# A two-layer graph network: 500 more tiles of edges counted in stage two, stored blocks' products placed early

## The chip, the cores and the metric

The kernel runs on one core of a Trainium2 chip. It is judged by its device time in microseconds, the median of several executions.

## What is computed

The graph has 12500 nodes with 128 features and 400000 edges, sorted by destination; a destination is 12500 times the square of a uniform number, so low nodes have most edges. Cut to what matters:

```python
def _mean_agg(h, src, dst, deg_inv):
    summed = jax.ops.segment_sum(h[src], dst, num_segments=N_NODES)
    return summed * deg_inv[:, None]
def _sage_conv(h, src, dst, deg_inv, W_self, W_neigh, b):
    return h @ W_self + _mean_agg(h, src, dst, deg_inv) @ W_neigh + b
h = jax.nn.relu(_sage_conv(x, src, dst, deg_inv, W_self1, W_neigh1, b1))
x = _layernorm(x + _sage_conv(h, src, dst, deg_inv, W_self2, W_neigh2, b2))
ef = (jax.nn.relu(edge_attr @ We1 + be1) @ We2 + be2) * jax.nn.sigmoid(ts @ Wt + bt)
msg = jax.nn.relu(jnp.concatenate([x[row], ef], axis=1) @ Wn1 + bn1) @ Wn2 + bn2
out = _layernorm(x + x + jax.ops.segment_sum(msg, col, num_segments=12500))
```

## The kernel before

Three stages run one after the other, with prefixes in the profile's names: `sum_x_` (sums over neighbours of x, then the nodes' first layer), `sum_z_` (the same with z, the first layer's result in the form of the second), `messages_` (the edges' part). The edges stand in tiles of 128, 3125 of them, five tiles to a group, 625 groups.

**Two ways to sum.** *Gathered* groups: POOL fetches for each tile 128 rows of the table by index (L954, an indirect DMA of 64 KB), DVE makes a one-hot matrix of destinations in a window of 64 nodes (L855), PE multiplies both (L1040, in fp32, which is two passes a tile), and DVE adds the window to `sums` (L1170). *Counted* tiles: the first 1250 (`COUNTED`), with the most edges for a node, are cut into 17 blocks. For every block a matrix is made that counts how often each of its up to 128 nodes has each source node: DVE makes two one-hot matrices of a tile (L1225 by destination and upper part of the source, up to 5 nodes x 98 columns; L1220 by its lower seven bits, five tiles at a time), PE multiplies them (L1051), DVE adds what the tile before left in a shared column (L1236, the carry), and ACT copies the result into `counts` (L1121). ACT clears these first (L1110). When a block is complete its counts are multiplied with the whole table: 98 matmuls with 384 columns (385 in stage 1), since the table is split into three bf16 parts (L1064). The table streams through a ring of three chunks, 14 chunks a product (L1014). The product is copied (ACT L1154), turned with six matmul passes (PE L1072) and added (DVE L1181).

**Stages.** Stage 1 (`counting=True`) counts the 1250 tiles, stores each block's counts in DRAM (3136 KB each) and gathers the other 375 groups. Stage 2 makes no counts: it loads the 17 stored ones (L1004, into two buffers in turn), multiplies them with its own table, and gathers the same 375 groups. Beside this, pieces of 256 nodes go through 15 steps each (`second_nodes` in stage 2: mean, two small products, layer norm, stores of y and rest), 49 pieces. Stage 3 gathers for all 625 groups; its edge indices `src_idx` and places `rel` are loaded and converted within stage 2.

**Order.** Nothing is scheduled by a program: every engine runs through slots `s = 0, 1, ...`, one for a group, and the plan (`make_plan`) says which tiles, products and pieces stand in a slot. Both stages have 375 groups and 401 slots. The tiles of stage 1 are spread over 340 slots by cost; in stage 2 a product takes 18 slots, one begins every 19 (`loaded_by`). POOL may be ten groups ahead of PE: it waits for `sums_ready`, which PE raises after a group's last window. SP issues all loads in program order and stands at a chunk until PE has freed one of the three. Within a slot PE mixes windows, counts and product evenly (lines 1079 to 1095).

## Time and profile before

| | us |
|---|---|
| Median of 3 executions | 10677.33 (10667.98 to 10677.83) |
| The profiled execution, in all | 10652.36 |
| Its span | 10648.5 |
| Granted TensorE clock, mean | 0.725 of full speed |

Busy in the whole span: PE 58%, PEld 46% (weight loads, beside PE), DVE 36%, ACT 25%, POOL 61%. The three stages lie one behind the other in the trace: stage 1 ends at 3099, stage 2 at 5888, stage 3 with the span. A busy POOL means an indirect DMA being written (0.94 us each); the time between two of them does not count as busy, though 0.30 us of it is always there. The clock and the DMA share must be read by stretch, since stage 2 differs from the other two.

### The profile page before, as it was taken

The numbers are of one execution on the slowest core, as the hardware profiler recorded it, in microseconds if no ns is written. First come the engines' busy times: TensorE is split into PE (matmuls) and PEld (weight loads), VectorE is DVE, ScalarE is ACT, GpSimd is POOL, SyncE is SP. The second block draws the span as 40 slices with busy tenths as digits, with TensorE's granted clock in tenths as the row PEclk, the third lists the DMA queues.
The fourth block names the chain that finished last, engine by engine and source line by source line (L and its number), as shares of the span: only waits on it lengthen the run. The fifth ranks groups of instructions, "written<-read, shape, count | busy, mean of one in ns | idle before, by whom it ended". The sixth has DMA issues, their size and how long they took to land. (4 is left out here: it accounts for less than half of the span.)

```text
span 10648.5 us, 114426 instructions
## 1 busy us (share of the span) xinstructions
PE 6164.5 (58%) x31767; PEld 4857.4 (46%) x31767; DVE 3810.3 (36%) x9118; ACT 2663.4 (25%) x3928; POOL 6516.8 (61%) x6882
## 2 busy tenths in 40 slices
PE   3456566666643334444444567666766667676676
PEld 2344444444433333343333455545555555555555
DVE  6766666666520111111111223233333333333333
ACT  3433333333200000000000233333333333333333
POOL 5555556566646666666665566666666666666665
PEclk9855666777756666666665788888888878888888
DMA  2334444555524444444432333333333333333332
GB/s 71 88 98 124 125 141 152 156 163 179 175 93 144 158 135 148 150 152 148 152 102 56 112 109 109 110 110 110 111 111 110 112 111 113 112 113 119 107 122 91
DMA packets 568848, 1305.10 MB, mean 123 GB/s; under 512 B 161231, under 2 KB 374499, under 8 KB 547476
## 3 DMA queue, kind: packets, MB, share of 16 engines
q1 hardware_dynamic: 348209, 846.63, 23.4%
q0 software_dynamic: 220000, 451.00, 15.7%
q8 instruction: 273, 4.47, 0.2%
q14 instruction: 366, 3.00, 0.1%
HBM read 1190.99 MB, written 106.10 MB: 122 GB/s over the span
## 5 line engine op out<-in xcount | busy, mean ns | idle before, releaser
L1465 POOL DMA_INDIRECT messages_rows<-y_d,src_idx x3125 | 2948.0, 943 | 1825.8 <-issue 955.4
L954 POOL DMA_INDIRECT sum_x_rows<-in_x,sum_x_edges x1875 | 1792.3, 956 | 1238.3 <-issue 532.5
L954 POOL DMA_INDIRECT sum_z_rows<-z_d,sum_z_edges x1875 | 1775.2, 947 | 1022.3 <-issue 536.0
L1509 PE MATMUL messages_p_msg<-Wm_e,messages_gated 128*128 128x128 f32 x6250 | 1102.5, 337 | 1046.1 <-DVE messages_gated L1573 941.0
L1509 PEld LDWEIGHTS messages_p_msg<-Wm_e,messages_gated 128*128 128x128 f32 x6250 | 961.7, 238 | 1373.6 <-DVE messages_gated L1573 1068.5
L1040 PE MATMUL sum_z_win<-sum_z_hot,sum_z_rows 128*128 128x64 f32 x3750 | 829.9, 330 | 1073.6 <-DVE sum_z_sums L1170 636.9
L1040 PEld LDWEIGHTS sum_z_win<-sum_z_hot,sum_z_rows 128*128 128x128 f32 x3750 | 894.7, 276 | 1153.3 <-DVE sum_z_sums L1170 677.2
L1568 DVE TENSOR_TENSOR messages_rows<-messages_p_msg,messages_rows 128x640 f32<-128x640 f32 x625 | 515.0, 824 | 2046.0 <-remote 1367.1
L1121 ACT CAST sum_x_counts<-sum_x_build 128x294 f32 (+3 forms) x1250 | 778.3, 623 | 1838.3 <-DVE sum_x_build L1236 1154.4
L1523 PEld LDWEIGHTS messages_win<-messages_hot,messages_rows 128*128 128x128 f32 x6250 | 864.6, 208 | 488.9 <-issue 431.8
L1051 PE MATMUL sum_x_build<-sum_x_key_hot,sum_x_low_hot 128*128 128x294 bf16 (+3 forms) x1250 | 508.3, 407 | 940.3 <-ACT sum_x_counts L1121 547.3
L1040 PEld LDWEIGHTS sum_x_win<-sum_x_hot,sum_x_rows 128*128 128x128 f32 x3750 | 931.6, 277 | 235.7 <-issue 174.9
L1523 PE MATMUL messages_win<-messages_hot,messages_rows 128*128 128x64 f32 x6250 | 841.1, 286 | 313.6 <-DVE messages_sums L1563 210.3
L1516 PE MATMUL messages_p_edge<-messages_hid,We 128*128 128x320 f32 x2500 | 956.3, 514 | 0.0
L1538 ACT ACTIVATE messages_hid<-messages_p_hid,be 128x640 f32<-128x640 f32 x625 | 494.2, 791 | 1824.2 <-remote 1304.5
L1040 PE MATMUL sum_x_win<-sum_x_hot,sum_x_rows 128*128 128x64 f32 x3750 | 867.6, 335 | 83.3 <-DVE sum_x_hot_sum L1200 47.9
L1170 DVE TENSOR_TENSOR sum_z_sums<-sum_z_sums,sum_z_win 128x64 f32 x375 | 83.3, 222 | 2224.8 <-DMA x_parts_d<-sum_x_split 1699.1
L1064 PE MATMUL sum_z_p_prod<-sum_z_split,sum_z_counts 128*128 128x384 bf16 x1666 | 689.5, 429 | 206.0 <-issue 96.6
L1546 ACT ACTIVATE messages_rows<-messages_rows 128x640 f32<-128x640 f32 x625 | 458.9, 734 | 1318.0 <-DVE messages_rows L1568 1060.9
L1573 DVE SCALAR_TENSOR_TENSOR messages_gated<-messages_p_edge,be,messages_gate 128x640 f32<-128x640 f32 x625 | 550.8, 881 | 472.6 <-remote 212.2
L1064 PE MATMUL sum_x_p_prod<-sum_x_split,sum_x_counts 128*128 128x385 bf16 x1666 | 642.5, 430 | 61.5 <-DMA sum_x_split<-x_parts_d 23.7
L1236 DVE SCALAR_TENSOR_TENSOR sum_x_build<-sum_x_counts,sum_x_build 128x98 f32<-128x98 f32 x1233 | 398.7, 323 | 780.5 <-ACT sum_x_counts L1121 233.5
(175 smaller groups left out, 6820.3 us busy)
## 6 DMA issues: line engine op xcount, KB each, us to landing
messages_when<-in_edge_weight SPq DMA_DIRECT2D x125, 1600.0 KB
sum_x_split<-x_parts_d SPq DMA_DIRECT2D x238, 675.5 KB
sum_z_split<-z_parts_d SPq DMA_DIRECT2D x238, 672.0 KB
messages_attr<-in_edge_attr SPq DMA_DIRECT2D x125, 800.0 KB
counts_d<-sum_x_counts SPq DMA_DIRECT2D x17, 3136.0 KB
sum_z_counts<-counts_d SPq DMA_DIRECT2D x17, 3136.0 KB
messages_rows<-y_d,src_idx POOLq DMA_INDIRECT x3125
sum_x_rows<-in_x,sum_x_edges POOLq DMA_INDIRECT x1875
```

The costliest lines, as they stand in the source:

```text
L954: nc.gpsimd.indirect_dma_start(out=rows[:, s % depth, j, :], out_offset=None, in_=table, in_offset=bass.IndirectOffsetOnAxis(ap=edges[:, b ...
L1040: last = nc.tensor.matmul(win[g % 2][:, 0:WIN], rows[:, g % depth, j, :], hot[:, q, j, :], start=j == 0, stop=j == TILES - 1)
L1051: nc.tensor.matmul(build[u % BUILDS][:, 0:columns], low_hot[:, u % LOWS, :], key_hot[:, u % HOTS, 0:columns], start=True, stop=True).then_ ...
L1064: last = nc.tensor.matmul(p_prod[:, 0:summed], by_count[b % 2][:, hi, :], split[:, n % XCHUNKS, hi % CHUNK, 0:summed], start=hi == 0, stop ...
L1121: nc.scalar.copy(by_count[b % 2][:, :, ds(column, w)], build[u % BUILDS][:, 0:w * plan.his].rearrange("p (n h) -> p h n", h=plan.his)).the ...
L1465: nc.gpsimd.indirect_dma_start(out=rows[:, g % DEPTH, j, :], out_offset=None, in_=d["y"], in_offset=bass.IndirectOffsetOnAxis(ap=t.src_idx ...
L1509: last = nc.tensor.matmul(msg[:, j * P:(j + 1) * P], gated[:, g % GATEDS, j * P:(j + 1) * P], t.Wm_e[:], start=True, stop=True)
L1516: last = nc.tensor.matmul(p_edge[:, h, 0:HALF], t.We2[:], hid[:, g % HIDS, h, :], start=True, stop=True)
L1523: last = nc.tensor.matmul(win[:, 0:WIN], rows[:, g % DEPTH, j, :], hot[:, g % WINDOW_HOTS, j, :], start=j == 0, stop=j == TILES - 1)
L1538: nc.scalar.activation(hid[:, g % HIDS], p_hid[:, :, 0:HALF], ACT.Relu, bias=t.be1[:, 0:1]).then_inc(hid_ready, 1)
L1568: nc.vector.tensor_tensor(at, msg[:, 0:GROUP], at, ALU.add).then_inc(msg_added, 1)
L1573: nc.vector.scalar_tensor_tensor(gated[:, g % GATEDS, :].rearrange("p (h c) -> p h c", h=2), p_edge[:, :, 0:HALF], t.be2[:, 0:1], gate[:, ...
```

## The change

Stage 2 now takes part in the counting. The first plan is the same as before; a second one (`make_plan` with begin and end) covers tiles 1250 to 1750.

- **Tiles.** 500 tiles leave stage 2's gathered groups: 275 are left of 375, 1375 gathers of 1875. They are counted in 16 new blocks, without storing. 100 of them span up to 5 nodes; the other 400 span 6, which is more than 490 columns, so each has a second unit of 98 columns, without a carry. 900 units in all are spread over 245 slots, two or three a slot for the first 40 slots, four afterwards.
- **Products.** Stage 2 has 33 (17 stored, 16 new) with 385 columns (the 385th sums the counts, as in stage 1): 3234 matmuls, before 1666, and 462 loads of chunks of 675.5 KB, before 238 of 672. Their order is 0, 1, 2, 17, 3, 4, 18, 5, 6, 19, and so on: two stored with each new one. A stored product has 3 slots, the next one begins 2 or 3 slots behind it: product 0 in slots 4 to 6, 1 in 9 to 11, 2 in 15 to 17, 17 in 20 to 22. The 24th is done by slot 132. The last nine, of new blocks, come 13 to 15 slots apart up to slot 253.
- **Buffers.** Stored counts have one buffer in place of two (`counts[2]`, loaded when the stored product before is done); the other two hold the new blocks. Gather buffers: 8 in place of 10. `second_nodes` uses two PSUM banks in place of four, with three more waits on PE (for `x1_copied`, `y_ready`, `rest_ready`) and its bias step one slot later, and loads pieces 2 slots ahead in place of 6.
- **Pieces.** 17 lie flat in `sums` before a ring of 8 (before 9), they start 4 slots apart at least (before 5), and stage 2 has 298 slots in place of 401.
- **Ends.** Stage 2 begins with the places of its blocks on DVE (`place_blocks`, some 45 small dependent operations) and has its checks in slot 2 and a total at its end. `src_idx` and `rel` are now loaded at the start of stage 3, first for 25 groups, for which POOL waits, and converted there. In stage 1, z is stored with two columns of ones more, and the preparation is split in two functions.

```diff
-COUNTED = 1250
-BLOCKS = 17
-WIDTHS = ((300, 2), (640, 3), (940, 4), (COUNTED, 5))
 WIDEST = 5
-CLEAR_OF = P - WIDEST
-COUNTED_BY = 340
-FLAT = 9
 RING = 8
-SPACING = 5
+SPACING, SPACING_SECOND = 5, 4
 PIECE_STEPS = 15
 CHUNK = 7
 SPLITS = 3
 XCHUNKS = 3
 HOTS, LOWS, BUILDS = 10, 20, 3
-DEPTH_COUNTING, DEPTH = 10, 10
+HOTS_SECOND, LOWS_SECOND, BUILDS_SECOND = 8, 10, 2
+DEPTH_FIRST, DEPTH_SECOND, DEPTH = 10, 8, 10
 EDGES_AHEAD, EDGES_RING = 4, 8
 WINDOW_HOTS = 4
 LOADS = 2
 HIDS, GATES, GATEDS = 3, 4, 3
 THIRD_STEPS = 10
+SOON = 25
...
+    plan.units = []
+    for b in plan.built:
+        for tile in range(plan.block_at[b], plan.block_at[b + 1]):
+            width = next(w for until, w in widths if tile < until)
+            plan.units += [(tile - begin, o, min(width - o, WIDEST), b) for o in range(0, width, WIDEST)]
...
+    plan.product_by = {}
+    if before:
+        ends = [4] + [plan.block_end[b] for b in plan.built]
+        left = list(range(plan.loaded))
+        for j, from_ in enumerate(ends):
+            now = [left.pop(0)] if left and j < blocks else []
+            now += [plan.built[j - 1]] if j else []
+            now += [left.pop(0)] if left and j < blocks else []
+            length = (ends[j + 1] - from_) // len(now) - 2 if j < blocks else 7
+            for i, b in enumerate(now):
+                plan.product_by[b] = (from_ + i * (length + 2), length)
+        assert not left
+    else:
+        for b in plan.built:
+            from_ = plan.block_end[b]
+            plan.product_by[b] = (from_, min(26, plan.block_end[b + 1] - from_ - 2) if b + 1 < plan.blocks else 9)
+    plan.products = sorted(plan.product_by, key=lambda b: plan.product_by[b])
...
-    plan = make_plan(m)
+    first = make_plan(m, 0, 1250, 17, 9, 340, ((300, 2), (640, 3), (940, 4), (1250, 5)), SPACING)
+    second = make_plan(m, 1250, 1750, 16, 17, 245, ((1350, 5), (1750, 6)), SPACING_SECOND, first)
...
+            wait_for(pe, x1_copied, n)
...
-        if s == 4:
+        if s == 5:
             i, before = turn(n)
             pe.wait_ge(inv_in[i], before * 32 + 32)
             wait_for(pe, rest_ready, n)
+            wait_for(pe, y_ready, n)
...
+            pe.wait_ge(rest_ready, n + 1)
...
-    side.load_ahead, side.ahead = load_ahead, 6
+    side.load_ahead, side.ahead = load_ahead, 2
...
+    depth = DEPTH_FIRST if first else DEPTH_SECOND
+    hots, lows, builds = (HOTS, LOWS, BUILDS) if first else (HOTS_SECOND, LOWS_SECOND, BUILDS_SECOND)
...
+    counts = [sb(f"counts{i}", [P, plan.his, P // 2], FP32) for i in range(3 if plan.loaded else 2)]
...
-                    for b, (at, length) in enumerate(product_by):
-                        if s == (0 if b < 2 else sum(product_by[b - 2])):
-                            wait_for(sp, split_used, plan.chunks * (b - 1))
-                            sp.dma_start(counts[b % 2][:], d["counts"][b]).then_inc(counts_in[b % 2], 16)
-                    if s == 60:
-                        sp.dma_start(t.src_idx[:].rearrange("p g j -> p (g j)"), d["src_tiles"]).then_inc(keep_in, 16)
-                        sp.dma_start(t.rel[:].bitcast(I32), d["dst_tiles"].rearrange("p (g j) -> p g j", j=TILES)).then_inc(keep_in, 16)
+                    for b in range(plan.loaded):
+                        if s == (0 if b == 0 else plan.done_at[b - 1]):
+                            wait_for(sp, split_used, plan.chunks * (plan.turn_of[b - 1] + 1) if b else 0)
+                            sp.dma_start(counts_of(b)[:], d["counts"][b]).then_inc(counts_in, 16)
+                for n, k, step in pieces_at[s + side.ahead] if s + side.ahead < last_slot else []:
+                    if step == 0:
+                        side.load_ahead(sp, n, k)
+                for n, k, step in pieces_at[s]:
+                    side.sync(sp, n, k, step)
                 for n in split_loads[s]:
-                    if counting:
+                    if first:
                         for i in range(2):
                             sp.wait_ge(split_stored[i], 16 * plan.chunks // 2)
                     wait_for(sp, split_used, n - XCHUNKS + 1)
                     c = n % plan.chunks
                     sp.dma_start(split[:, n % XCHUNKS], parts[:, c * CHUNK:(c + 1) * CHUNK, :]).then_inc(split_in[n % XCHUNKS], 16)
-                for n, k, step in pieces_at[s + side.ahead] if s + side.ahead < last_slot else []:
-                    if step == 0:
-                        side.load_ahead(sp, n, k)
-                for n, k, step in pieces_at[s]:
-                    side.sync(sp, n, k, step)
             side.sync_last(sp)
...
             def product_step(b, hi):
-                n = b * plan.chunks + hi // CHUNK
+                turn = plan.turn_of[b]
+                n = turn * plan.chunks + hi // CHUNK
                 if hi == 0:
-                    wait_for(pe, sums_added, block_added[b - 1] if b else 0)
-                    if counting:
-                        pe.wait_ge(copied, plan.block_at[b + 1])
+                    wait_for(pe, sums_added, block_added[plan.products[turn - 1]] if turn else 0)
+                    if b < plan.loaded:
+                        pe.wait_ge(counts_in, 16 * (b + 1))
                     else:
-                        pe.wait_ge(counts_in[b % 2], 16 * (b // 2 + 1))
+                        pe.wait_ge(copied, plan.unit_end[b])
                 if hi % CHUNK == 0:
                     pe.wait_ge(split_in[n % XCHUNKS], 16 * (n // XCHUNKS + 1))
-                last = nc.tensor.matmul(p_prod[:, 0:summed], by_count[b % 2][:, hi, :], split[:, n % XCHUNKS, hi % CHUNK, 0:summed],
+                last = nc.tensor.matmul(p_prod[:, 0:summed], by_count(b)[:, hi, :], split[:, n % XCHUNKS, hi % CHUNK, 0:summed],
                                         start=hi == 0, stop=hi == plan.his - 1)
                 if hi % CHUNK == CHUNK - 1:
                     last.then_inc(split_used, 1)
...
+                    if o == 0:
+                        act.wait_ge(cleared, CLEARS * (b - plan.loaded + 1))
+                    act.wait_ge(built, i + 1)
+                nc.scalar.copy(by_count(b)[:, :, ds(column + o, w) if o else ds(column, w)],
+                               build[i % builds][:, 0:w * plan.his].rearrange("p (n h) -> p h n", h=plan.his)).then_inc(copied, 1)
...
         def _(dve):
-            if counting:
+            if first:
                 begin.vector(dve)
-                dve.wait_ge(begin.bases_ready, 4)
+            placed.vector(dve)
+            dve.wait_ge(placed.bases_ready, 4)
...
-                    if s == 80:
-                        dve.wait_ge(keep_in, 32)
-                        nc.vector.tensor_copy(t.rel[:], t.rel[:].bitcast(I32)).then_inc(keep_ready, 1)
-                        dve.wait_ge(keep_ready, 1)
-                    if s == 81:
-                        nc.vector.tensor_tensor(t.rel[:], t.rel[:], t.fast_base[:].unsqueeze(2).to_broadcast([P, m.NG, TILES]),
-                                                ALU.subtract).then_inc(keep_ready, 1)
...
+                if g in (0, SOON):
+                    pool.wait_ge(keep_in[1 if g else 0], 32)
...
+            for i, part in enumerate(kept):
+                columns = slice(part.start * TILES, part.stop * TILES)
+                sp.dma_start(t.src_idx[:, part].rearrange("p g j -> p (g j)"), d["src_tiles"][:, columns]).then_inc(keep_in[i], 16)
+                sp.dma_start(t.rel[:, part].rearrange("p g j -> p (g j)").bitcast(I32), d["dst_tiles"][:, columns]).then_inc(keep_in[i], 16)
+                if i == 0:
+                    load_body(0)
...
+            def own_places(i):
+
+                part = kept[i]
+                dve.wait_ge(keep_in[i], 32)
+                nc.vector.tensor_copy(t.rel[:, part], t.rel[:, part].bitcast(I32)).then_inc(rel_ready, 1)
+                dve.wait_ge(rel_ready, 2 * i + 1)
+                nc.vector.tensor_tensor(t.rel[:, part], t.rel[:, part],
+                                        t.fast_base[:, part].unsqueeze(2).to_broadcast([P, part.stop - part.start, TILES]),
+                                        ALU.subtract).then_inc(rel_ready, 1)
+                dve.wait_ge(rel_ready, 2 * i + 2)
+
+            own_places(0)
...
+                if s == SOON // 2:
+                    own_places(1)
```

On PE at the first product of stage 2, before (`sum_z_win` is a window of a gathered tile, `p_prod` the product):

```order
L1040 MATMUL sum_z_win<-sum_z_hot,sum_z_rows 128x64
L1064 MATMUL sum_z_p_prod<-sum_z_split,sum_z_counts 128x384
L1040 MATMUL sum_z_win<-sum_z_hot,sum_z_rows 128x64
L1064 MATMUL sum_z_p_prod<-sum_z_split,sum_z_counts 128x384 x2
L1040 MATMUL sum_z_win<-sum_z_hot,sum_z_rows 128x64
```

The same place after, where product 0 begins (`sum_z_build` is a unit of counts):

```order
L1145 MATMUL sum_z_build<-sum_z_key_hot,sum_z_low_hot 128x490
L1133 MATMUL sum_z_win<-sum_z_hot,sum_z_rows 128x64
L1159 MATMUL sum_z_p_prod<-sum_z_split,sum_z_counts 128x385 x6
L1133 MATMUL sum_z_win<-sum_z_hot,sum_z_rows 128x64
L1145 MATMUL sum_z_build<-sum_z_key_hot,sum_z_low_hot 128x490
L1159 MATMUL sum_z_p_prod<-sum_z_split,sum_z_counts 128x385 x7
L1133 MATMUL sum_z_win<-sum_z_hot,sum_z_rows 128x64
L1159 MATMUL sum_z_p_prod<-sum_z_split,sum_z_counts 128x385 x6
L1133 MATMUL sum_z_win<-sum_z_hot,sum_z_rows 128x64
```

Six or seven product matmuls stand between two windows, where one or two stood.

On SP, the loads around the first products, before (x4 is four chunks in a row):

```order
L966 DMA sum_z_edges<-in_edges 128x50 x4
L1004 DMA sum_z_counts<-counts_d 128x6272 x2
L1014 DMA sum_z_split<-z_parts_d 128x2688
L966 DMA sum_z_edges<-in_edges 128x50
L1014 DMA sum_z_split<-z_parts_d 128x2688 x4
L966 DMA sum_z_edges<-in_edges 128x50
L1014 DMA sum_z_split<-z_parts_d 128x2688 x4
```

And after:

```order
L1064 DMA sum_z_edges<-in_edges 128x50 x3
L1101 DMA sum_z_counts<-counts_d 128x6272
L1064 DMA sum_z_edges<-in_edges 128x50
L1113 DMA sum_z_split<-z_parts_d 128x2702 x14
L1068 DMA sum_z_counted<-in_edges 128x50
L1064 DMA sum_z_edges<-in_edges 128x50
L1101 DMA sum_z_counts<-counts_d 128x6272
L1113 DMA sum_z_split<-z_parts_d 128x2702 x14
L1064 DMA sum_z_edges<-in_edges 128x50
L1101 DMA sum_z_counts<-counts_d 128x6272
L1113 DMA sum_z_split<-z_parts_d 128x2702 x10
```

All 14 chunks of a product now stand together, and each stored block's counts stand ahead of its chunks and behind the last chunk of the stored product before; loads of edges stand between such runs.

## Rows read from the trace of the kernel before

**Rows 1.** The page, part 5, stage 2: busy, mean ns | idle, releasers.
```profile
L1040 PE MATMUL sum_z_win<-sum_z_hot,sum_z_rows 128*128 128x64 f32 x3750 | 829.9, 330 | 1073.6 <-DVE sum_z_sums L1170 636.9
...
L1064 PE MATMUL sum_z_p_prod<-sum_z_split,sum_z_counts 128*128 128x384 bf16 x1666 | 689.5, 429 | 206.0 <-issue 96.6
```

**Rows 2.** Windows: PE, PEld, DVE, ACT, POOL busy; PEclk, DMA share, GB/s.
```profile
3204.00:3704.00 500.00, 191.62 (x1085) 175.55 (x1083) 54.65 (x188) 4.72 (x10) 325.84 (x347) 0.61 0.45 144
...
5204.00:5704.00 500.00, 202.90 (x1056) 185.62 (x1055) 81.50 (x290) 8.66 (x25) 324.15 (x343) 0.59 0.36 104
```

**Rows 3.** Waits of POOL, 3204 to 5204: total us, times, longest.
```profile
POOL sum_z_rows L954 <- DMA x_parts_d<-sum_x_split: 266.5, 84, 6.3
```

**Rows 4.** Timeline of POOL: start, duration, engine, line, operation [idle before].
```profile
3333.80 0.94 POOL L954 DMA_INDIRECT sum_z_rows<-z_d,sum_z_edges  x1 [4.57 <-DMA x_parts_d<-sum_x_split]
3335.05 0.94 POOL L954 DMA_INDIRECT sum_z_rows<-z_d,sum_z_edges  x1 [0.30 <-issue]
...
3369.97 0.94 POOL L954 DMA_INDIRECT sum_z_rows<-z_d,sum_z_edges  x1 [5.29 <-DMA x_parts_d<-sum_x_split]
```

**Rows 5.** Timeline of POOL: first, last gather of stage 2, first of stage 3.
```profile
3104.13 0.94 POOL L954 DMA_INDIRECT sum_z_rows<-z_d,sum_z_edges  x1 [71.34 <-DMA sum_z_edges<-in_edges]
...
5829.27 0.94 POOL L954 DMA_INDIRECT sum_z_rows<-z_d,sum_z_edges  x1 [0.30 <-issue]
5888.31 0.94 POOL L1465 DMA_INDIRECT messages_rows<-y_d,src_idx  x1 [58.09 <-issue]
```

**Rows 6.** Timeline of PE in stage 2, at low and at high clock.
```profile
3334.37 0.53 PE L1064 MATMUL sum_z_p_prod<-sum_z_split,sum_z_counts 128*128 128x384 bf16 x1
...
3335.01 0.53 PE L1064 MATMUL sum_z_p_prod<-sum_z_split,sum_z_counts 128*128 128x384 bf16 x1
...
4200.15 0.33 PE L1064 MATMUL sum_z_p_prod<-sum_z_split,sum_z_counts 128*128 128x384 bf16 x1
...
4200.48 0.33 PE L1064 MATMUL sum_z_p_prod<-sum_z_split,sum_z_counts 128*128 128x384 bf16 x1
```

**Rows 7.** Windows at the start of stage 2, columns as in rows 2.
```profile
3115.00:3120.00 5.00, 1.10 (x6) 1.13 (x6) 0.00 (x0) 0.00 (x0) 3.78 (x5) 0.50 1.01 431
...
3130.00:3140.00 10.00, 1.35 (x13) 1.07 (x11) 0.00 (x0) 0.00 (x0) 7.56 (x9) 0.80 0.21 53
```

**Rows 8.** The page, DMA issues: KB of each.
```profile
sum_z_split<-z_parts_d SPq DMA_DIRECT2D x238, 672.0 KB
...
sum_z_counts<-counts_d SPq DMA_DIRECT2D x17, 3136.0 KB
```

**Rows 9.** Line groups of stage 1 2400 to 2970; columns as in rows 1.
```profile
L1121 ACT CAST sum_x_counts<-sum_x_build 128x490 f32 x157 | 110.1, 702 | 299.1 <-DVE sum_x_build L1236 190.5 <-issue 102.3 <-PE sum_x_build L1051 6.3
L1225 DVE TENSOR_TENSOR sum_x_key_hot<-iota_ps,sum_x_key 128x490 bf16<-128x490 f32 x153 | 99.6, 657 | 0.0
L1051 PE MATMUL sum_x_build<-sum_x_key_hot,sum_x_low_hot 128*128 128x490 bf16 x156 | 73.2, 469 | 86.4 <-ACT sum_x_counts L1121 42.1 <-issue 17.0 <-DVE sum_x_key_hot L1225 16.1
```

**Rows 10.** Windows late in stage 1, columns as in rows 2.
```profile
2000.00:2500.00 500.00, 314.43 (x1485) 218.09 (x1483) 323.15 (x727) 171.38 (x283) 303.76 (x321) 0.75 0.53 165
```

**Rows 11.** Timeline of DVE in stage 1: two carries in a row.
```profile
2604.07 0.33 DVE L1236 SCALAR_TENSOR_TENSOR sum_x_build<-sum_x_counts,sum_x_build 128x98 f32<-128x98 f32 x1 [0.56 <-issue]
...
2605.61 0.32 DVE L1236 SCALAR_TENSOR_TENSOR sum_x_build<-sum_x_counts,sum_x_build 128x98 f32<-128x98 f32 x1
```

**Rows 12.** Line groups of PE from 3600 to 4800: pieces and flips.
```profile
L778 PE MATMUL sum_z_piece_p_y<-Wm_x,sum_z_piece_x1T 128*128 128x128 f32 x76 | 20.0, 358 | 27.8 <-issue 27.8
...
L1072 PE MATMUL sum_z_p_prod<-identity,sum_z_product 128*128 128x128 f32 x48 | 13.1, 446 | 62.1 <-ACT sum_z_product L1154 36.5 <-issue 25.6
```

**Rows 13.** Timeline of DVE: stage 1's block places; conversion for stage 3.
```profile
7.18 0.81 DVE L241 CAST counted_base<-counted_base 128x1250 f32<-128x1250 int32 x1 [1.43 <-DMA counted_base<-in_tile_first]
...
22.35 0.27 DVE L663 MEMSET sum_x_piece_hB<- 23x256 f32 x1 [0.16 <-issue]
...
3743.01 3.41 DVE L1280 TENSOR_TENSOR rel<-rel,fast_base 128x3125 f32<-128x3125 f32 x1
```

More of the change, by code:

```diff
@@ new lines, in make_plan @@
+    assert plan.chunks * CHUNK == plan.his and begin % BODY == 0 and end % BODY == 0 and (tiles - end) % BODY == 0
+    plan.loaded = before.blocks if before else 0
+    plan.blocks = plan.loaded + blocks
+    low, high = (begin / tiles) ** 2, (end / tiles) ** 2
+    edges_of = [round(tiles * sqrt(low + (high - low) * b / blocks)) for b in range(blocks + 1)]
+    plan.block_at = (before.block_at[:-1] if before else []) + edges_of
+    assert plan.block_at[plan.loaded] == begin and plan.block_at[-1] == end
@@ new lines, in make_plan @@
+    plan.built = range(plan.loaded, plan.blocks)
+    plan.units = []
[3 more added lines that the diff above has]
+            plan.units += [(tile - begin, o, min(width - o, WIDEST), b) for o in range(0, width, WIDEST)]
+    plan.widest = max(o + w for _, o, w, _ in plan.units)
+    plan.clear_of = P - plan.widest
+    plan.unit_end = {b: sum(1 for unit in plan.units if unit[3] <= b) for b in plan.built}
@@ L105, in make_plan @@
             plan.last_block.append(last)
[L106 removed]
+            ready.append(max(plan.done_at[b] for b in range(from_, last + 1)) + 2)
         else:
             tile = tiles * sqrt(min((PIECE * (k + 1) + 80) / m.N, 1.1))
[L109 removed]
+            ready.append(min(int((tile - end) / TILES) + 4, plan.groups + 2))
     plan.order, plan.start, slot = [], {}, 0
@@ L121, in make_plan @@
         slot = max(slot, last + 2)
-        plan.third.append(slot)
+        starts.append(slot)
         slot += SPACING
-    assert [k for k in plan.order if k >= FLAT] == list(range(FLAT, m.PIECES))
-    assert plan.start[FLAT] < plan.start[FLAT - 2]
-    return plan
+    return starts
 def by_slot(slots, items):
@@ L903, in sum_neighbours @@
     for k, b in enumerate(plan.last_block):
-        assert sum(product_by[b]) + 1 <= plan.start[k] + 2
-    if counting:
+        assert max(plan.done_at[i] for i in range(plan.first_block[k], b + 1)) + 1 <= plan.start[k] + 2
+    own_tables = Names()
+    own_tables.counted_base, own_tables.column = sb("counted_base", [P, plan.tiles], FP32), sb("column", [1, plan.tiles], I32)
+    own_tables.place_int, own_tables.again = sb("place_int", [1, plan.groups], I32), sb("again_now", [1, 1], I32)
+    own_tables.block_int = t.block_int if first else sb("block_int", [1, len(plan.built)], I32)
```

609 lines of the change are left out of this document (328 added, 281 removed).

## Prediction

> **What bounds the kernel now.** I read the page first, then stage 2 by windows, then POOL's waits and timeline, and last the engines that POOL waits for. Stage 2 lasts from its first gather at 3104.13 us to the first gather of stage 3 at 5888.31 [rows 5], 2784 us. Its 1875 gathers end at 5829.27, so they take 2725 us, 7.27 us for a group of five, and the tail behind them takes 59 us. Every part of the stage keeps that pace: 347 gathers in 500 us with products, 343 in the window in which the last products end [rows 2]. POOL alone would be quicker: one gather starts 1.25 us after the other (3333.80 and 3335.05), which is 6.25 us for a group. But between 3333.80 and 3369.97 only 25 gathers start, 36.2 us in place of 31.2, since POOL stands still for about 5 us once in 25 [rows 4]. From 3204 to 5204 such stops make 267 us in 84 waits [rows 3]. The releaser named there, an old transfer of stage 1, cannot be it: what POOL waits for is the semaphore by which PE frees gather buffers, and I take it that PE's completions come late in bunches. PE is busy for 192 and 203 of 500 us [rows 2], and both its windows and its product matmuls overlap in that (mean 330 and 429 ns, far longer than their distance below) [rows 1]; DVE is busy for 11 to 16%, DMA for 36 to 45% of its time. So the stage is set by the number of groups times some 7.3 us, POOL first, PE behind it, and nobody else is near.
>
> **What the change removes.** 500 tiles are 100 groups of 375. At 7.27 us these are 727 us of gathers, the whole possible gain. The products of the stored blocks stay, 17 of them, and the tail stays: its last pieces wait for the last groups as before, and the plan leaves 8 slots between the last group and the last piece's start where there were 11, so I take 55 us (50 to 60).
>
> **What it adds to the first half.** Slots 4 to 132 now hold 24 products (17 stored, 7 new), one for 5.33 slots, where there was one for 19. At gather pace 5.33 slots are 38.8 us. Three things have to fit in.
> *Transfers.* A product reads 14 chunks of 675.5 KB (672 before [rows 8]), 9.68 MB. While two counts and three chunks were loaded the queues moved 431 GB/s at a share of 1.01, and 53 with gathers alone [rows 7], so 378 are free for loads: 25.6 us for a product. A stored one also needs its counts, 3136 KB [rows 8], 8.5 us, and 17 of 24 are stored: 6.0 us on average. Together 31.6 of 38.8 us. There is one buffer for stored counts, and SP issues the next load only when the product before has ended, but the gap of two slots (14.5 us) covers 8.5.
> The engines' limit is where the Trainium skill speaks against the change: "DMA: Bandwidth & Descriptors", section "Where 436 GB/s comes from", says that for traffic between HBM and SBUF a per-core limit of about 358 GB/s binds. The 431 GB/s of the trace [rows 7] disagree. By the page's figure a product would take 39.2 us of transfers, 7.6 us more than by the row, nothing would be left for gaps, and the sum would be some 24 x 7.6 = 180 us higher.
> *PE.* At the low clock a product's matmul and a tile's two passes follow each other every 0.64 us (3334.37 to 3335.01), at the high one every 0.33 [rows 6]: 0.32 us for one of the two at 1.2 GHz. For 5.33 slots that makes 98 + 27 = 125 of them, 40.0 us; 13 matmuls of counts by 0.469, their mean busy time in stage 1 [rows 9], 6.1; a third more than one piece, some 16 small matmuls by 0.358, 5.7; six flips by 0.446 [rows 12], 2.7. In all 54.5 us at 1.2 GHz, 27 at 2.4 GHz. Which clock? Stage 2 had 0.59 to 0.61 with PE at 40% [rows 2]; late stage 1, whose mix is nearest to the new one, had 0.75 with PE at 63% [rows 10]. At 0.75 the work is 36 us, just under the 38.8 of the gathers.
> *The stops.* If PE's late completions come once in so many of its instructions, they grow with these: about 90 in five slots before (50 window, 27 product, the rest pieces and flips), about 170 now. Then the 5 us become 10, and five slots take 41.2 us, 44 for a product.
> So POOL (33.3 us of its own work), PE (36) and DMA (31.6) are each near the pace, and coupled by a ring of three chunks and now 8 gather buffers where there were 10 (50 to 58 us of lead). I take 46 us for a product: 44 by the stops, 2 for chunks that come late. The bounds are 38.8 (all hidden) and 60 (PE near the low clock all the time, 54.5, and a stop of 5). 24 x 46 = 1104 us.
>
> **The second half.** Slots 132 to 275 hold 143 groups, nine products of new blocks, 4 units a slot and most of the pieces. The nearest row is late stage 1, which counted about three tiles a slot and had 321 gathers in 500 us, 7.79 us for a group, with DVE busy at 65% [rows 10]. Here it is 2.2 tiles a slot, two units each, the second one of 98 columns and without a carry. A carry follows the last after 1.54 us [rows 11], the sum of 0.66 (DVE one-hot, or PE 0.47) and 0.70 on ACT [rows 9], partly overlapped; with the small unit I estimate 2 us for a tile, 4.4 of 7.3 us. So the chain of counts fits, and so does DVE. I take 7.6 us (7.27 to 7.9): 1087 us.
>
> **The ends.** Stage 2 now begins with some 45 small dependent operations on DVE, and as many checks in slot 2. Stage 1's ran from 7.18 to 22.35 us [rows 13], 15 us. POOL does not wait for them, it can run 8 groups ahead; what shows is that PE starts late and has to catch up: 15 us (0 to 40). The first four slots: 4 x 7.27 = 29 us. Stage 3 now begins with the load of the first 25 groups' indices, for which POOL waits, and two operations on 128 x 3000 elements, one of which is 3.41 us long on 128 x 3125 [rows 13]; both were hidden in stage 2. I take 8 us (3 to 15), since POOL's buffers cover the second. Stage 1 keeps its plan number for number; one memset, and pieces that store two more columns: nothing (the 7.79 us a group hide it, uncovered it would be below 1 us a piece).
>
> **Sum.** 15 + 29 + 1104 + 1087 + 55 + 8 = 2298 us for what took 2784: 486 less. The profiled execution took 10652.4 us (span 10648.5), 25 below the median of 10677.3. 10652 - 486 + 25 = 10,191 us, say 10,190.
>
> **Rivals.**
> *All hidden.* The clock rises with the work, PE stays under the pace, the stops stay as they are. For it: PE at 2.4 GHz needs 27 of 38.8 us, DMA 31.6. Against: late stage 1, with PE no busier, lost 0.5 us a group. 275 x 7.27 + 5 + 50 + 3 = 2057, 727 less: 9,950 us.
> *A product is the pace.* SP waits for a chunk to be free in the middle of its queue, and the counts, the edges and the pieces' loads stand behind it; if DMA idles through these waits and PE is at 0.6 as in stage 2, the work is 45 us of PE plus 10 of stops and 5 for the counts that come late: 60. Then 24 x 60 = 1440, 336 more than in the sum: with 7.9 us a group in the second half (43 more) and 32 at the ends 10,600, without these 10,530.
> *Slower than before.* One mechanism: PE does not leave 1.2 GHz and its late completions scale with its instructions, in slots 4 to 132. 54.5 + 10 for the stops, and every stored product waits the 8.5 us for its counts with PE standing, as 12.5 us of stops would: 71 us on average. The break-even is where 15 + 29 + 24p + 1087 + 55 + 8 = 2784, p = 66 us. At 71 it is 10,790. Against it: no long window of the trace has PE busy at over 60% and a clock at 0.5.
> *It doesn't do what it says.* If PE's share of the pace per group is what counts and merely moves, the 100 groups less bring nothing where products are: that is the second rival again, and the second half still gains.
>
> **Chances.** The forecast (42 to 53 us a product) 0.50, all hidden 0.18, a product is the pace 0.20, slower 0.08, left over 0.04. The range leaves out the extremes of both sides: 9,970 to 10,570. What a measurement of this kernel can tell from no change is about 0.2%, 21 us: faster 0.88, within 0.03, slower 0.09.
>
> **What would show it.** In the new profile: 1375 gathers in stage 2; from its start to the end of the 24th product about 1150 us with gathers at 8.6 us a group, a PE clock of about 0.75, and DMA at 300 GB/s and over; then 7.6 us a group at a higher share of DVE; a tail of 55 us; stage 1 and 3 within 15 us of before. Wrong would be: waits of PE for counts or chunks above 5 us a product (second rival), a clock of 0.5 to 0.6 beside a busy PE (third), POOL at 7.2 us a group all through (first), or a second half at over 8 us.

## The result and the profile after

The changed kernel takes 10433.85 us (10424.62 to 10438.49, 4 executions), the kernel before 10672.65 (10662.69 to 10677.83, 4). The ratio is 0.9776, with a 95% interval of 0.9759 to 0.9793: 239 us less. The forecast was 10,190 in 9970 to 10,570, 487 less than the 10,677 it started from. The direction and the range held; the gain is half of the forecast, and that half is the subject of what follows.

By stages, from the first and the last gathers of the profiled executions ([rows 5] before; the 100 groups that leave, 727 us before, have no row of their own):

| | before | forecast | after |
|---|---|---|---|
| stage 1, until stage 2's first gather | 3104 | 3104 | 3130 |
| stage 2, slots 0 to 4 | | 44 | 25 |
| slots 4 to 132 (24 products) | 931 at 7.27 | 1104 | 1290 |
| slots 132 to 275 | 1040 at 7.27 | 1087 | 1176 |
| tail | 59 | 55 | 51 |
| stage 2 in all | 2784 | 2290 | 2542 |
| stage 3, to the end of the span | 4760 | 4768 | 4765 |
| span | 10648.5 | | 10436.9 |

POOL's timeline after the change (start, duration, line, operation; the idle time in brackets), which answers to [rows 5]:

```profile
3130.43 0.94 POOL L1052 DMA_INDIRECT sum_z_rows<-z_d,sum_z_edges  x1 [74.59 <-DMA sum_z_edges<-in_edges]
...
5621.10 0.94 POOL L1052 DMA_INDIRECT sum_z_rows<-z_d,sum_z_edges  x1 [0.30 <-issue]
5672.29 0.95 POOL L1570 DMA_INDIRECT messages_rows<-y_d,src_idx  x1 [50.24 <-DMA rel<-in_dst_tiles]
```

The two halves by windows (columns as in [rows 2]: PE, PEld, DVE, ACT, POOL busy; clock, DMA share, GB/s). The first one is slots 4 to 132, 641 gathers in 1290 us, 10.1 us a group; in the second a group takes 8.2:

```profile
3159.00:4449.00 1290.00, 813.95 (x4288) 538.72 (x4289) 462.66 (x1405) 351.19 (x555) 605.42 (x641) 0.78 0.74 254
4449.00:5621.00 1172.00, 634.86 (x3240) 506.30 (x3240) 453.67 (x1416) 347.49 (x569) 673.46 (x711) 0.67 0.45 134
```

The clock is 0.78 in the first half, as forecast (0.75), so PE has more time, not less. DMA's share is 0.74, with 254 GB/s. No engine and no queue is busy all the time, and the pace is still 40% worse than before (10.1 us a group for 7.27). The waits of that first half (in all, times, longest) name who is late:

```profile
POOL sum_z_rows L1052 <- PE sum_z_win L1133: 480.1, 88, 12.3
...
PE sum_z_p_prod L1159 <- DMA sum_z_split<-z_parts_d: 197.6, 173, 6.7
...
PE sum_z_build L1145 <- ACT sum_z_counts L1217: 126.1, 48, 11.9
```

POOL waits 480 us for PE ([rows 3] had 267 in a window of 2000), and PE waits 198 us for chunks of the table. One such place in the timeline, PE's product matmuls and POOL's gathers beside them:

```profile
3425.14 0.67 PE L1159 MATMUL sum_z_p_prod<-sum_z_split,sum_z_counts 128*128 128x385 bf16 x3 [1.28 <-DMA sum_z_split<-z_parts_d]
...
3427.15 0.67 PE L1159 MATMUL sum_z_p_prod<-sum_z_split,sum_z_counts 128*128 128x385 bf16 x3 [0.32 <-DMA sum_z_split<-z_parts_d]
...
3429.10 0.50 PE L1159 MATMUL sum_z_p_prod<-sum_z_split,sum_z_counts 128*128 128x385 bf16 x2 [0.23 <-DMA sum_z_split<-z_parts_d]
...
3421.43 0.95 POOL L1052 DMA_INDIRECT sum_z_rows<-z_d,sum_z_edges  x1 [0.30 <-issue]
3428.79 0.95 POOL L1052 DMA_INDIRECT sum_z_rows<-z_d,sum_z_edges  x1 [6.41 <-PE sum_z_win L1133]
```

PE takes 7 matmuls of a chunk, and the next chunk's first comes 2.0 us after this chunk's first, though 7 matmuls and a tile's window are 1.3 us of work at this clock (they start 0.16 us apart). POOL meanwhile stands for 6.4 us, since the windows that free its buffers come behind the chunk in PE's program order. Over the whole product (matmuls 1 to 98 of products 1 to 22, from the trace) 35.5 us pass on average, and 18.6 to the next: 54 us, where 46 were forecast. The page's groups of stage 2 (busy, mean | idle before, releasers), beside [rows 1]:

```profile
L1052 POOL DMA_INDIRECT sum_z_rows<-z_d,sum_z_edges x1375 | 1301.7, 947 | 1264.5 <-PE sum_z_win L1133 686.8
...
L1159 PE MATMUL sum_z_p_prod<-sum_z_split,sum_z_counts 128*128 128x385 bf16 x3234 | 870.2, 384 | 241.6 <-DMA sum_z_split<-z_parts_d 218.3
...
L1145 PE MATMUL sum_z_build<-sum_z_key_hot,sum_z_low_hot 128*128 128x490 bf16 (+1 forms) x900 | 332.5, 369 | 560.2 <-ACT sum_z_counts L1217 358.6
```

POOL was idle for 1264 us before 1375 gathers, with PE as the main releaser, and nine tenths of PE's idle time before a product's matmul are waits for a chunk (218 of 242). Before counts' matmuls PE waits for ACT (359 of 560), which copies the unit before last: there are two PSUM buffers for units.

### The profile page after: what moved, and what is told of

It is laid out like the page before. It is cut to its first block and busy times, and to the rows that moved or that the text cites. A ratio compares the mean times of both kernels' runs of the same rounds, so it can differ in the third digit from the quotient of the medians.

```text
span 10436.9 us, 126206 instructions
## 1 busy us (share of the span) xinstructions
PE 6538.4 (63%) x33333; PEld 4906.0 (47%) x33333; DVE 4362.5 (42%) x10662; ACT 3339.5 (32%) x4956; POOL 6056.9 (58%) x6382
## 5 line engine op out<-in xcount | busy, mean ns | idle before, releaser
L1052 POOL DMA_INDIRECT sum_z_rows<-z_d,sum_z_edges x1375 | 1301.7, 947 | 1264.5 <-PE sum_z_win L1133 686.8
L1217 ACT CAST sum_x_counts<-sum_x_build 128x294 f32 (+3 forms) x1250 | 779.9, 625 | 1857.9 <-DVE sum_x_build L1341 1163.3
L1217 ACT CAST sum_z_counts<-sum_z_build 128x490 f32 (+1 forms) x900 | 578.1, 656 | 1586.9 <-DVE sum_z_build L1341 667.9
L1159 PE MATMUL sum_z_p_prod<-sum_z_split,sum_z_counts 128*128 128x385 bf16 x3234 | 870.2, 384 | 241.6 <-DMA sum_z_split<-z_parts_d 218.3
L1133 PEld LDWEIGHTS sum_z_win<-sum_z_hot,sum_z_rows 128*128 128x128 f32 x2750 | 641.3, 260 | 163.1 <-issue 112.5
L1145 PE MATMUL sum_z_build<-sum_z_key_hot,sum_z_low_hot 128*128 128x490 bf16 (+1 forms) x900 | 332.5, 369 | 560.2 <-ACT sum_z_counts L1217 358.6
## 6 DMA issues: line engine op xcount, KB each, us to landing
sum_z_split<-z_parts_d SPq DMA_DIRECT2D x462, 675.5 KB
sum_x_split<-x_parts_d SPq DMA_DIRECT2D x238, 675.5 KB
```

Of the source, the lines that this page charges most:

```text
L1052: nc.gpsimd.indirect_dma_start(out=rows[:, s % depth, j, :], out_offset=None, in_=table, in_offset=bass.IndirectOffsetOnAxis(ap=edges[:, b ...
L1133: last = nc.tensor.matmul(win[g % 2][:, 0:WIN], rows[:, g % depth, j, :], hot[:, q, j, :], start=j == 0, stop=j == TILES - 1)
L1145: nc.tensor.matmul(build[i % builds][:, 0:columns], low_hot[:, u % lows, :], key_hot[:, i % hots, 0:columns], start=True, stop=True).then_ ...
L1159: last = nc.tensor.matmul(p_prod[:, 0:summed], by_count(b)[:, hi, :], split[:, n % XCHUNKS, hi % CHUNK, 0:summed], start=hi == 0, stop=hi ...
L1217: nc.scalar.copy(by_count(b)[:, :, ds(column + o, w) if o else ds(column, w)], build[i % builds][:, 0:w * plan.his].rearrange("p (n h) -> ...
```

## The experiments

All of them ran on chips on which the kernel before takes 9055 to 9070 us and not 10,673; what differs is taken up below. There are four such chips, and they agree: beside e1 to e4 the kernel before took 9055 us, beside e5 to e8 9057, beside e9 9070, beside e10 and e11 9057. In what follows "the second chip" stands for any of them and "the first chip" for where the first two traces were taken; that it was another chip is inferred from the times. Each ratio is to the kernel before on the same chip. Microseconds against e6 go across chips for e1 to e4, which is good to some 3 us, and for e9 the ratios are compared.

**e5: the kernel before, unchanged.**

> The kernel before as it is, for its trace on the chip on which the next kernels run. Where the chip shows POOL's stops (5 us once in 25 gathers, as in the trace before the change), a group of stage two takes 7.27 us and the whole 10,650; where it does not, as in the four traces taken so far of changed kernels, 6.25 us a group, stage two 375 x 6.25 + 60 = 2400 us and the whole about 9055. Every theory gives the same here.

9060 us, as expected of a chip without the stops. POOL's stops are gone: 398 gathers in 500 us where [rows 2] had 347, and two of the 1875 gathers of stage 2 start more than 1.6 us behind the one before.

```profile
2957.00:3457.00 500.00, 285.63 (x1294) 248.00 (x1295) 76.92 (x253) 7.20 (x17) 378.99 (x398) 0.59 0.53 173
```

A group takes 6.25 us from the stage's start to its last gather, and the stage 2380 us (2757.2 to 5136.9).

**e6: the changed kernel, unchanged.**

> The changed kernel as it is. On a chip with the stops: 0.978 of the kernel before, as recorded. On one without: the 24 early products take 50 us each all the same (theory A: the stream of chunks does not depend on the stops), 9.5 us a group, the second half 6.25 us a group: stage two 63 + 1220 + 940 + 40 = 2250, 150 off, 0.983 or a little more. If the stops were the reason for most of the missing gain, 100 groups less would bring 625 us, 0.93.

0.9707 (0.9691 to 0.9723), 263 us less than before; stage 2 takes 2123, 257 less, and everything else is the same within 4 us. So the gain in microseconds is nearly the one of the first chip (239). 100 groups less are worth 625 us here at 6.25, and 370 of them are given back:

```profile
2778.00:3938.00 1160.00, 794.89 (x4274) 526.69 (x4274) 459.35 (x1401) 349.67 (x554) 603.60 (x641) 0.82 0.82 282
3938.00:4836.00 898.00, 598.05 (x3307) 472.15 (x3306) 461.06 (x1441) 346.84 (x571) 676.07 (x716) 0.75 0.58 176
```

The first half takes 1160 us, 9.1 us a group in place of 6.25; the second 898, 6.28 us a group, POOL's own pace. The expectation had 2250 us for the stage and 0.983; it took 63 us for the start (25 measured), 1220 for the first half and 940 for the second. The waits of the first half are those of the first chip:

```profile
POOL sum_z_rows L1052 <- PE sum_z_win L1133: 380.6, 78, 9.1
...
PE sum_z_p_prod L1159 <- DMA sum_z_split<-z_parts_d: 229.8, 200, 6.0
...
PE sum_z_p_prod L1167 <- ACT sum_z_product L1252: 48.6, 23, 4.4
PE sum_z_build L1145 <- ACT sum_z_counts L1217: 47.0, 35, 5.7
```

A product takes 34.3 us here (35.5 there), 2.45 us a chunk. Between two products 15.5 us pass. In this half PE never waits for gathered rows, and POOL is seven to eight groups ahead of it at the end of a product and at the end of a gap alike: PE is the one behind all the time. In the second half it is the other way round:

```profile
PE sum_z_win L1133 <- DMA sum_z_rows<-z_d,sum_z_edges: 156.9, 65, 5.7
...
POOL sum_z_rows L1052 <- PE sum_z_win L1133: 7.5, 14, 1.6
```

**e1: short loads.**

```diff
-                    sp.dma_start(split[:, n % XCHUNKS], parts[:, c * CHUNK:(c + 1) * CHUNK, :]).then_inc(split_in[n % XCHUNKS], 16)
+                    some = CHUNK if first or n < XCHUNKS else 1
+                    sp.dma_start(split[:, n % XCHUNKS, 0:some], parts[:, c * CHUNK:c * CHUNK + some, :]).then_inc(split_in[n % XCHUNKS], 16)
```

> Stage two's chunk loads, behind the first three, bring one of their seven rows (96 KB in place of 675 KB); all matmuls, counts and waits stay, and the products are wrong. The changed kernel took 1293 us for slots 4 to 132 (24 products, 53.9 us each, 10.1 us a group) and 1170 us for slots 132 to 275 (8.2 us a group). Theory A (the chunks: in a stored product's three slots 14 chunks come at 2.4 us each and PE stands for them, windows and counts behind it): the first part falls to 8.2 us a group or less, 24 x 44 = 1050, so 240 us off the whole (about 10,190), the second part by under 30. Theory B (PE's own work at a clock of 0.77 is the pace): under 60 us off. Theory C (the counting chain DVE, ACT, PE with two build buffers): some 60 us off in the first part, nothing in the second.

0.9404 (0.9389 to 0.942), 278 us less than e6. All of it comes from the first half, 877 us in place of 1160; the second is within 4 us:

```profile
2778.00:3655.00 877.00, 717.96 (x4273) 520.78 (x4273) 459.08 (x1401) 349.07 (x554) 603.90 (x640) 0.83 0.52 156
3655.00:4548.00 893.00, 618.63 (x3308) 485.23 (x3306) 461.06 (x1441) 347.06 (x571) 675.38 (x715) 0.73 0.33 86
```

PE does the same 4273 matmuls, and waits 20 us for chunks in place of 230; POOL waits 94 us for PE in place of 381:

```profile
POOL sum_z_rows L1052 <- PE sum_z_win L1134: 94.3, 60, 4.9
...
PE sum_z_p_prod L1160 <- DMA sum_z_split<-z_parts_d: 20.4, 16, 3.7
```

A product takes 22.8 us, of which PE is busy for 22.4: without the waits for chunks, PE's work is what a product lasts. That is theory A, and with more than it expected. Short loads also leave the queues freer for the gathers and the counts, so this run alone does not say which of the two helped; e7 does.

**e9: fewer matmuls in a product, all loads.**

```diff
+                if not first and hi % CHUNK % 2 and hi % CHUNK != CHUNK - 1:
+                    return
                 last = nc.tensor.matmul(p_prod[:, 0:summed], by_count(b)[:, hi, :], split[:, n % XCHUNKS, hi % CHUNK, 0:summed],
```

The products are incomplete here. The kernel compares the total of the counts with what it should be (`vector_again`) and would turn to its slow general path; that comparison was made one that never does, here and in e2 and e10.

> Stage two's products make 56 of their 98 matmuls (four of seven for a chunk), all loads and waits stay; the products are wrong. It tells PE's work from the stream of chunks, which the short loads left open, since they also take DMA work from the gathers. Theory A (the round trip of three chunks sets a product): a product stays at 33 to 35 us and the whole within 40 us of the changed kernel (0.971 of before on a chip without stops). Theory B (PE's matmuls are on the path too): 42 matmuls less at 0.17 to 0.32 us are 7 to 13 us a product, 170 to 320 us off, 0.94 to 0.95.

0.968 (0.9664 to 0.9697), where e6 had 0.9707 (0.9691 to 0.9723). The first half takes 1131 us in place of the 1160 of e6, a product 33.1 us in place of 34.3. 42 of 98 matmuls are worth 1.2 us a product. With e1 this closes the matter from both sides: a product lasts as long as its chunks take to arrive, and PE's work in it is under that.

**e7: a ring of four chunks.**

```diff
-    split = sb("split", [P, XCHUNKS, CHUNK, wide], BF16)
+    ring = XCHUNKS if first else 4
+    split = sb("split", [P, ring, CHUNK, wide], BF16)
```

and `ring` for `XCHUNKS` where chunks are loaded and used (four semaphores in `split_in`).

> A ring of four chunks in stage two in place of three, nothing else. Theory A, sharpened: a product's 14 chunks take 34 us, 2.4 us each, in every trace with full loads, although the queues could bring one in 1.8 us; with three buffers a chunk has 7.3 us from being freed to being used again. With four, if that round trip stays, 1.8 us a chunk: 26 to 28 us a product, 24 x 7 = 170 us less than the changed kernel of this call. If instead the queues themselves deliver no more than 285 GB/s beside the gathers, no change (within 20 us).

0.9556 (0.954 to 0.9572), 139 us less than e6. A product takes 28.7 us, 2.05 a chunk, the first half 1025 us:

```profile
2778.00:3803.00 1025.00, 758.15 (x4275) 510.13 (x4275) 459.22 (x1401) 349.89 (x554) 604.28 (x641) 0.83 0.87 319
```

```profile
POOL sum_z_rows L1053 <- PE sum_z_win L1134: 244.7, 71, 6.7
...
PE sum_z_p_prod L1160 <- DMA sum_z_split<-z_parts_d: 129.4, 149, 7.2
```

The queues deliver 319 GB/s over this half with the same loads and the same gathers, against 282 in e6. So with three buffers it is the round trip, not the queues, that sets 2.45 us a chunk: 3 x 2.45 = 7.3 us from one use of a buffer to its next, and 4 x 2.05 = 8.2 with four. The expectation had taken that the 7.3 us stay, which would have given 1.8 us a chunk and 170 us; the round trip grew by 0.9 us instead, with DMA's share at 0.87 for 0.82. Since the gathers here share the queues with more traffic, not less, e7 also settles what e1 left open.

**e2: no units of counts.**

```diff
-    units_at = by_slot(last_slot, [(s, i) for i, s in enumerate(plan.slot_of)])
+    units_at = by_slot(last_slot, [(s, i) for i, s in enumerate(plan.slot_of)] if first else [])
```

With this the loads of the counted tiles' edges go too, and PE, before a new block's product, waits for the clearing of its counts in place of the last copy.

> Stage two makes no units of counts: no one-hot matrices for them, no matmuls, carries and copies; the new blocks' counts are cleared and multiplied all the same, with all loads, so the sums lack 500 tiles. Theory C (the chain of counts sets the second half): slots 132 to 275 fall from 8.2 to 7.3 us a group, 125 us off, and the first half by 0.5 us a group, 60 off, in all 180 (about 10,250). Theory A: the first half stays within 60 us of 1293. Theory B (PE's work): both halves fall in proportion to PE's busy time, about 10 to 15%, 300 us off.

0.9635 (0.9619 to 0.9651), 74 us less than e6. The first half takes 1082 us in place of 1160, the second 892 in place of 897. The expectation of 180 was made with the first chip's second half in mind; on this chip the chain of counts costs 5 us in the whole second half, and 0.6 us a group in the first. Theory C is out as the main cause: without any unit the first half still takes 8.5 us a group.

**e4: ten gather buffers.**

```diff
-DEPTH_FIRST, DEPTH_SECOND, DEPTH = 10, 8, 10
+DEPTH_FIRST, DEPTH_SECOND, DEPTH = 10, 10, 10
```

> Ten gather buffers in stage two in place of eight, as before the change, nothing else. If POOL's stops come from the shorter lead (58 us of gathers then, 73 now at 10 us a group with ten), 50 us or more off. If PE is behind all the time, as theories A to C say, the buffers are full whatever their number and only the start gains: 0 to 20 us off, within 0.2%.

0.97 (0.9684 to 0.9716), 8783 us beside 8794 in e6: no difference that can be told from none, as expected where PE is behind POOL all the time.

**e3: one stored product with each new one.**

```diff
-            now = [left.pop(0)] if left and j < blocks else []
+            now = [left.pop(0)] if j == 0 else []
             now += [plan.built[j - 1]] if j else []
             now += [left.pop(0)] if left and j < blocks else []
```

> The same work in another place: one stored product goes with each new one in place of two, so the 33 products are spread over slots 4 to 253, stored ones over 3 to 7 slots; the number of slots stays 298. Theory A: no product asks for chunks faster than one in 3 us, the waits for them go and every slot takes about 8.3 us: 275 x 8.3 = 2283 against 2491 now, 200 us off (about 10,230). Theory B (PE's work in all is the pace): same work, same time, within 40 us. Theory C: likewise within 60 us.

0.9428 (0.9412 to 0.9444), 254 us less than e6 with the same work and the same 298 slots: slots 4 to 132 take 831 us in place of 1160, slots 132 to 275 969 in place of 897. A product still takes 36.1 us, but over five or six slots in place of three, for which POOL needs 31 to 38 us anyway: it waits 42 us for PE in the first half, where it waited 381. This undoes just what the title says, that the stored ones come early, and it is worth about as much as the whole change (263).

**e8 and e11: spread, ring of four, ten buffers.**

> Three edits together: one stored product with each new one, a ring of four chunks, ten gather buffers. On a chip without stops stage two then can come near POOL's own pace: 275 x 6.3 + 45 = 1780 us, and the whole 60 to 90 us under the spread kernel alone (which took 0.943 of the kernel before): 0.935. On a chip with stops: 0.955, since the stops stay at 7.3 us a group and more.

> Spread products, a ring of four, ten buffers once more. On a chip with stops: no slot has more than 12 to 18 product matmuls, the pace is that of the stops, 7.3 to 8 us a group, 10,150 to 10,250 where the kernel before takes 10,670. On a chip without them 8437 again.

The edits are those of e3, e7 and e4 together; both runs are the same kernel. 0.9315 (0.93 to 0.9331), 8437 us, and 8434.6 in e11. Both halves run at 6.25 us a group, POOL's own pace:

```profile
2778.00:3578.00 800.00, 605.48 (x3680) 441.19 (x3681) 465.47 (x1421) 353.78 (x562) 604.85 (x641) 0.84 0.85 304
3578.00:4471.00 893.00, 661.43 (x3903) 497.59 (x3901) 453.48 (x1422) 341.54 (x562) 675.50 (x714) 0.79 0.78 270
```

Stage 2 takes 1760 us; 275 x 6.25 + 41 of tail are 1760, so nothing of the counting and of the 33 products is left on the path. The three edits leave the 275 gathered groups and the tail as the only limit. It beats both kernels. How much of it remains on a chip with POOL's stops was not seen: e11 too ran on one without.

**e10: no units, again.**

> The kernel without units once more, for the case that this call meets a chip with POOL's stops: there the second half of stage two took 8.2 us a group with units. If it falls to 7.3 without them, the units lengthen the stops (more instructions on PE, ACT and DVE between two of them); if it stays at 8.2, it is the products and pieces. On a chip without stops it repeats 6.25 us a group in the second half and some 8720 in all.

8737.9 us (one execution), beside 9056.9 for the kernel before: a chip without stops, so it repeats e2 within 18 us, and the question stays open.

## Why the prediction was half right

**What is removed** held as a count: 375 groups became 275. What 100 groups are worth is their number times the pace before, 727 us on the first chip, 625 on the second.

**The chunks** are the term that failed: 2 us a product "for chunks that come late". The prediction divided 9.68 MB by the 378 GB/s that [rows 7] leave for loads and got 25.6 us for a product, 31.6 with counts, "of 38.8 us". That rate was read where two counts of 3136 KB and three chunks were queued together, so the queues were never empty. In a product only three chunks can be under way, and each is asked for when PE has used one up: about 2.5 us each, 34 to 36 us a product, on both chips, in e4, e2 and e3 alike, and 28.7 with a ring of four. The second half of the slip was to average over 5.33 slots: a product has three slots (21.8 us at 7.27), and PE works in program order, so the 35 us hold up the three groups' windows. The 2.33 slots behind them do not give it back, though POOL's rows lie ready there: they take 15.5 us in e6, in which PE is busy for 8.8 and waits for ACT's copy of the product (2.1), for ACT's copies of counts (2.1), for chunks (1.2) and for DVE's one-hot matrices (0.7), besides small waits of the pieces. A term by slots would have been 34 + 2.33 x 7.27 = 51 us. Measured: 35.5 + 18.6 = 54.1.

The forecast's 46 were 33.3 of POOL's own pace, 10.7 of stops that grow and 2 for chunks. On the second chip, where nothing stops, a product and its gap take 1160 / 24 = 48.3 us: 15.0 above POOL's own pace, where 2 stood. The first chip adds 130 us in this half, 5.4 a product, and it had added 1.02 us a group before the change (7.27 for 6.25), which is 5.4 a product too. By this estimate across chips the stops did not grow here, so the 5.3 us that the forecast added for their growth stood on a cause that did not come, and covered part of the one that did: 13.0 too little for the chunks, 5.3 too much for the stops, in all 7.8 a product or 186 us. That the range held is in part luck.

The rival "a product is the pace" named the mechanism (60 us a product, 10,530), and the result is nearer to it than to the forecast. But it priced a product by a PE clock of 0.6 and by counts that come late, which e9 and the clock of 0.78 to 0.82 do not bear out. Two of the signs of being wrong came: PE's waits for chunks are 8.2 us a product (198 in 24), and the second half takes over 8 us a group.

**The page's rule.** The Trainium skill ("DMA: Bandwidth & Descriptors", section "Where 436 GB/s comes from") says that for traffic between HBM and SBUF about 358 GB/s per core bind; from that the prediction estimated 39.2 us of transfers for a product. The trace does not agree: [rows 7] have 431 GB/s in 5 us, and 50 us of e7 have 372 as their mean:

```profile
3682.00:3732.00 50.00, 37.24 (x225) 24.02 (x226) 23.09 (x72) 15.89 (x27) 26.77 (x29) 0.90 0.97 372
```

In the first half of the changed kernel the mean is 254 GB/s, far below either figure; what bound there was the ring.

**PE** had the work that was summed, 36 us a product at a clock of 0.75: it was busy for 814 us in the first half, 34 a product at 0.78. It was not the pace of the products: e9.

**The second half**, 8.2 for 7.6 us a group on the first chip, is the other term that was mis-sized (89 us), and it is not the chain of counts by itself: in e6 the same instructions take 6.28 us a group. What differs is below.

**The start** cost POOL nothing (25 us for four groups in place of 44, its own pace): its buffers covered the block places. The tail (51 for 55) and stage 3 (4 us more for 8) held. Stage 1 took 26 us longer in the profiled execution of the changed kernel; in e5 and e6 it is 2757 and 2753, so the change does not cost it there.

**Slower than before** was far off: 54 us a product against a break-even of 66. The low clock did not appear, and PE's idle time before a product's first matmul, where the counts would be waited for, is 33 us for all 24 products of e6, 6.0 at most.

## The stops, which the chips do not share

The prediction took POOL's stops of 5 us in 36 as a part of the program. They are not: the same kernel in e5 has none. Its other stages are shorter too: stage 1 by 347 us, stage 2 by 404 and stage 3 by 841. (They are not as regular as that either: [rows 3] have 84 waits in 2000 us, 3.2 us each.) The prediction's reading, that PE's completions come late, is borne out by the traces. At the stop of [rows 4] PE's last matmul ends at 3325.75, and 7 us later all that wait for PE go on within 0.9 us: SP, which needs a free chunk, DVE with its add, and POOL at 3333.80:

```profile
3332.92 0.80 SPq L1014 DMA_DIRECT2D sum_z_split<-z_parts_d  x2
3333.19 0.22 DVE L1170 TENSOR_TENSOR sum_z_sums<-sum_z_sums,sum_z_win 128x64 f32 x1 [10.70 <-DMA x_parts_d<-sum_x_split]
```

Elsewhere POOL's lead hides the delay. Where the last matmul of a window ends at 3755.2, the add that needs it starts 16 us later, while POOL's gathers go on:

```profile
3754.88 0.33 PE L1040 MATMUL sum_z_win<-sum_z_hot,sum_z_rows 128*128 128x64 f32 x2
...
3771.12 0.22 DVE L1170 TENSOR_TENSOR sum_z_sums<-sum_z_sums,sum_z_win 128x64 f32 x1 [17.06 <-DMA x_parts_d<-sum_x_split]
```

On the second chip:

```profile
3367.06 2.37 PE L1040 MATMUL sum_z_win<-sum_z_hot,sum_z_rows 128*128 128x64 f32 x10 [7.77 <-DMA sum_z_rows<-z_d,sum_z_edges]
...
3369.63 0.22 DVE L1170 TENSOR_TENSOR sum_z_sums<-sum_z_sums,sum_z_win 128x64 f32 x1 [9.95 <-PE sum_z_win L1040]
```

Over the 375 groups of stage 2 before the change, the time from a window's last matmul to its add has a median of 6.9 us on the first chip, and one in ten is above 20.8; on the second the median is 0.20 and the longest 0.57. After the change, a copy of a unit's counts (L1217) begins more than 3 us behind its matmul in 119 of the last 450 units on the first chip and in 7 of 450 on the second. So on the first chip the chain from PE to DVE to ACT and back carries these delays, and the new chain of counts, four units a slot, adds a place for them; that fits 8.2 beside 6.28 us a group, but no kernel was run on such a chip that takes the units away, so it is argued, not shown. What makes the completions late stays open. Around 3755 the gathered rows had landed (2.1 to 4.0 us behind each gather's issue, by the trace's packets). PE's granted clock was still 1.00 from 3756 to 3757, after PE had stopped at 3755.2, and 0.50 from 3758 on, so at this place the clock fell after the stop had begun and did not cause it.

## What to carry to other kernels

A stream through a small ring runs at the ring's round trip, not at the queues' rate: take the time per chunk from a place where the same number of transfers is under way, and compare it with the time in which the consumer wants it, slot by slot, not as a mean over the gaps. Where an engine works in program order, work that could wait for data should be spread evenly between the work that others wait for; here placing the same products otherwise was worth 254 us, and the whole change 263. And before a term is built on a stop that recurs in a trace, see whether it is the program's or the chip's.

## What the runs showed of the hardware that was not expected

- The same kernel takes 10,673 us where the first traces were taken and 9055 to 9070 on four chips after that. Bare gathers have the same distance everywhere, 1.25 us; in stage 2 the difference is in what waits for PE.
- With three transfers of 675.5 KB (691,712 bytes) under way the queues brought one in 2.45 us (282 GB/s, beside some 15 gathers a product), with four one in 2.05 (338 GB/s), and at the start of stage 2, with more queued, at some 378 GB/s for 5 us (431 less the 53 of gathers [rows 7]).
- A PE that waits for chunks for 230 of 1160 us, busy for 69% of them, still was granted a clock of 0.82; one at 40% busy got 0.6 [rows 2].
